# Local attention in chunks of 32 queries by 64 keys, one step per pair of heads, with a shifted copy of V by DMA

## The reference

```python
        def local_attention(q, k, v):            # 16 heads of 64, WINDOW = 32
            ...
            bk2, bv2 = (look(bk), look(bv))      # window before and own window: 64 keys
            ...
            mask = (it < jb) | (it > jb + w) | (jb == -1)
            sim = jnp.einsum('bhwie,bhwje->bhwij', bq, bk2) * QK_SCALE
            sim = jnp.where(mask, -jnp.finfo(sim.dtype).max, sim)
            attn = jax.nn.softmax(sim, -1)
            out = jnp.einsum('bhwij,bhwje->bhwie', attn, bv2)
        ...
        for i in range(DEPTH):
            x = attn_layer(shift_tokens(x), Wqkv[i], q_scale[i], k_scale[i], Wo[i]) + x
            x = ffn_layer(shift_tokens(x), ln_g[i], ln_b[i], W1[i], b1[i], W2[i], b2[i]) + x
```

## Time and profile before

| | |
|---|---|
| median of the runs | 5675.37 us |
| profiled execution | 5674.6 us, its span 5672.5 us |
| PE, PEld busy | 5156.9 us (91%), 3769.0 us (66%) |
| DVE, ACT, POOL busy | 4207.5 us (74%), 4014.1 us (71%), 2657.0 us (47%) |
| the two stretches of local layers | about 1040 to 3280 us and 3500 to 5672 us |

### The profile page before, as it was taken

The page is one execution under the profiler, slowest core; times in us unless marked ns, Lnnn a source line. Parts: engine busy times, 40 slices in busy tenths (PEclk is TensorE's granted clock), DMA queues, the critical chain, the costliest instruction groups (busy, mean ns, idle before and its releaser), DMA issues. The chain is left out here.

```text
span 5672.5 us, 176489 instructions
## 1 busy us (share of the span) xinstructions
PE 5156.9 (91%) x68706; PEld 3769.0 (66%) x68706; DVE 4207.5 (74%) x6500; ACT 4014.1 (71%) x7192; POOL 2657.0 (47%) x2485
## 2 busy tenths in 40 slices
PE   8997995799999999999998899799999999999998
PEld 3334432587777777777776433687777777777776
DVE  7885655687777777777776788687777777777775
ACT  5784664577777777777776578677777777777775
POOL 1100100465566665566654110475656665656663
PEclk8996997899999999999999899899999999999999
DMA  0000000100000000000000000100000000000000
GB/s 13 2 2 6 2 2 9 35 20 15 19 17 18 21 17 20 16 21 19 17 21 13 4 2 2 37 19 16 20 18 16 23 16 21 15 21 17 17 22 18
DMA packets 129243, 89.14 MB, mean 16 GB/s; under 512 B 33396, under 2 KB 122000, under 8 KB 128376
## 3 DMA queue, kind: packets, MB, share of 16 engines
q1 hardware_dynamic: 128376, 77.32, 4.9%
HBM read 69.54 MB, written 1.05 MB: 12 GB/s over the span
## 5 line engine op out<-in xcount | busy, mean ns | idle before, releaser
L1746 POOL TENSOR_TENSOR cross<-raw,tab_b 128x512 f32<-128x512 f32 x768 | 998.5, 1324 | 298.8 <-ACT raw L1612 295.5
L737 DVE TENSOR_REDUCE arena<-PS 128x1 f32<-128x512 f32 (+3 forms) x1408 | 828.9, 648 | 215.9 <-PE PS L550 130.4
L1752 POOL CAST kT_b<-kT 128x512 bf16<-128x512 f32 x384 | 349.5, 910 | 1199.2 <-ACT kT L1668 1198.1
L688 ACT ACTIVATE arena<-PS 128x1024 f32<-128x1024 f32 (+1 forms) x704 | 668.8, 968 | 200.7 <-PE PS L573 124.2
L1838 DVE TENSOR_TENSOR rot<-PS,tab_a 128x512 f32<-128x512 f32 x768 | 522.7, 687 | 330.7 <-ACT raw L1612 172.0
L1612 ACT COPY raw<-PS 128x512 f32<-128x512 f32 x768 | 448.1, 592 | 270.2 <-PE PS L1463 224.1
L1861 DVE TENSOR_TENSOR rot<-rot,inv_norm 128x1024 f32<-128x1024 f32 x384 | 561.8, 1463 | 47.7 <-ACT inv_norm L1628 37.8
L1867 DVE TENSOR_TENSOR oT<-PS,rec_den 128x384 f32<-128x384 f32 (+1 forms) x576 | 298.8, 519 | 369.3 <-ACT rec_den L1646 369.0
L1854 DVE TENSOR_TENSOR rot<-rot,cross 128x1024 f32<-128x1024 f32 x384 | 560.0, 1458 | 14.9 <-POOL cross L1746 13.7
L1442 PE MATMUL PS<-PT,V 128*64 128x96 f32 x8448 | 484.4, 256 | 76.2 <-DVE oT L1867 60.6
L1463 PE MATMUL PS<-w_qk_high,x_high 128*128 128x256 f32 x1536 | 478.0, 311 | 79.0 <-issue 34.0
(11 more groups left out here) (260 smaller groups left out, 12668.8 us busy)
## 6 DMA issues: line engine op xcount, KB each, us to landing
w_qk<-in_w_pairs SPq DMA_DIRECT2D x196, 128.0 KB, 2.1
w_v<-in_w_pairs SPq DMA_DIRECT2D x100, 128.0 KB, 2.2
w_o<-in_w_out_pairs SPq DMA_DIRECT2D x192, 64.0 KB, 1.9
xs<-staged SPq DMA_DIRECT2D x24, 224.0 KB, 2.5
w<-in_L_ffn_W SPq DMA_DIRECT2D x12, 341.0 KB
q_parts<-max_rows SPq DMA_DIRECT2D x192, 2.0 KB
V<-in_c_E SPq DMA_DIRECT2D x2, 896.0 KB, 7.9
w<-in_L_ffn_W SPq DMA_DIRECT2D x24, 64.0 KB
```

The source lines that it names most:

```text
L688: nc.scalar.activation(PT[u % 6].rearrange("p (a n) -> p a n", a=2)[:, :, first_q:512], PS[:, 2 * (u % 2):2 * (u % 2) + 2, first_q:512], A ...
L737: nc.vector.tensor_reduce(maxima[:, 2 * m + h, qt, kh:kh + 1], bank[:, 0:keys_of(qt, kh)], AX.X, ALU.max).then_inc(bank_free, 1)
L1746: nc.gpsimd.tensor_tensor(dst[:, :, :, o:o + 32], src[:, :, :, other:other + 32], tab[:, :, o:o + 32].unsqueeze(2).broadcast_to([128, 8, 2 ...
```

## The change

- Chunks are 32 queries by 64 keys. Four products of 64 keys by 32 queries lie in the array's four tiles at once; a pair has 64 such score products and 64 for the values. The mask and maximum products are 64 x 64, 32 of them, in the same four tiles.
- All chunks of a pair fill banks 4 and 5 completely (512 columns each), so there is one step: one `exps` of 1024 columns per partition, values in banks 6 and 7, the sums in banks 4 and 5, one Ln, one Exp and one `quotients` of 1024 columns. PT, log_den and rec_den are single buffers. Nothing of a pair's attention is left for the next position but what waits for it.
- V is kept at whole tiles of 128 tokens: four pieces, not six, 8 chunks, not 11. The keys of the even 32-query windows are V moved down by 32 partitions: SP makes this copy, `V_early`, by two DMAs in each even position, after `split_v`, after V3 is copied and after the last reader of the buffer. `values` waits for them (`v_moved`) in odd positions.
- The maxima go over blocks of 64 queries by 96 keys, in two groups of four.
- The order: Y0 and Y1 move from slots 0 and 1 to 1 and 2; V pieces stand in slots 5 and 1; X1 moves from slot 3 to 2; `inverse_norm`, `square`, `norms` and `normalise` are placed anew on ACT and DVE.

```diff
-QC = 96
-CHUNKS = -(-N // QC)
+QC = 32
+UNITS = N // 128
-KB = 80
+KB = 96
...
+        V_early = [own(f"V_early{m}", [128, UNITS, 256]) for m in range(2)]
...
             if yy:
-                names += {0: ["Y0"], 1: ["Y1"]}.get(slot, [])
+                names += {1: ['Y0'], 2: ['Y1']}.get(slot, [])
...
+                            taken_apart(sp, l, b, p, "V3")
+                            need_apart(sp, pv_full, it - 2)
+                            sp.dma_start(V_early[j % 2][32:128, :, :], V[j % 2][0:96, :, :]).then_inc(v_moved, 16)
+                            sp.dma_start(V_early[j % 2][0:32, 1:UNITS, :], V[j % 2][96:128, 0:UNITS - 1, :]).then_inc(v_moved, 16)
...
+                    for m in range(UNITS):
+                        for t in range(2):
+                            for w in range(2):
+                                for h in range(2):
+                                    rows, at = slice(64 * h, 64 * h + 64), 128 * m + 64 * w + QC * t
+                                    last = nc.tensor.matmul(PS[64 * w:64 * w + 64, 4 + h, 64 * m + QC * t:64 * m + QC * t + QC], kT[par][rows, at:at + 64],
+                                                            qT[par][rows, at:at + QC], start=False, stop=True,
+                                                            tile_position=(64 * h, 64 * w), skip_group_check=True)
...
+                def values(l, b, p, r):
+                    pair = (p + 7) % 8
+                    need(pe, exp_done, r + 1)
+                    need(pe, o_done, r)
+                    if p % 2 == 1:
+                        need(pe, v_moved, (r + 2) * 16)
...
@@ PE, position @@
-                    if oo:
-                        values(r - 1, NS - 1, (p + 6) % 8)
                     if bb:
                         maximum(l, b, p, 0)
                         maximum(l, b, p, 1)
...
                     if bb:
-                        scores(l, b, p, r, 0)
+                        scores(l, b, p, r)
                     late(l, b, p, 1)
-                    for s in range(NS - 1):
-                        if bb:
-                            scores(l, b, p, r, s + 1)
-                            values(r, s, (p + 7) % 8)
-                        late(l, b, p, s + 2)
+                    if bb:
+                        values(l, b, p, r)
+                    late(l, b, p, 2)
+                    late(l, b, p, 3)
                     late(l, b, p, 4)
```

More of the change, by code:

```diff
@@ L48, in shape_constants @@
     out = {"c_ident": np.eye(128, dtype=np.float32)}
[L50 to L57, removed]
-    out["c_E"] = E.reshape(128, -1)
[L60 to L63, removed]
+    j, q = np.arange(64)[None, :], np.arange(QC)[:, None]
+    E = np.zeros((2, 64, UNITS + 1, 64), np.float32)
+    E[:, 0:QC, :, :] = np.where((j >= q) & (j <= q + 32), 0.0, NEG)[None, :, None, :]
+    for unit in range(UNITS):
+        E[:, QC + unit, unit, :] = 1.0
+    E[:, QC, UNITS, :] = 1.0
+    E[:, QC + UNITS, UNITS, 0:32] = NEG
+    out["c_E"] = E.reshape(128, -1)
+    turn = np.zeros((128, 2, 64), np.float32)
+    turn[i, :, i % QC] = 1.0
+    turn[i % 64 < QC, :, QC + UNITS] = 1.0
+    out["c_turn"] = turn.reshape(128, -1)
+    blocks = np.zeros((128, 5, KB), np.float32)
+    i64, j96 = np.arange(64)[:, None], np.arange(KB)[None, :]
+    near = (j96 >= i64) & (j96 <= i64 + 32)
+    for c in range(5):
         for u in range(2):
-            blocks[64 * u:64 * u + 48, c, :] = np.where(near & (j80 >= 32) if c == 0 and u == 0 else near, 0.0, NEG)
+            blocks[64 * u:64 * u + 64, c, :] = np.where(near & (j96 >= 32) if c == 0 and u == 0 else near, 0.0, NEG)
     out["c_blocks"] = blocks.reshape(128, -1)
@@ L1166, in window_layers @@
         ff_cols, b2_row = own("ff_cols", [128, 8]), own("b2_row", [128, C])
[L1167 to L1170, removed]
+        E = own("E", [128, UNITS + 1, 64], BF16)
+        half_mask = [own(f"half_mask{m}", [128, 5, KB], BF16) for m in range(2)]
+        R, max_parts = own("R", [128, 128], BF16), own("max_parts", [128, 128], BF16)
         norms2 = [own(f"norms2_{m}", [128, 16]) for m in range(2)]
@@ new lines, in scores @@
+                                nc.tensor.matmul(PS[64 * w:64 * w + 64, 4 + h, 64 * m:64 * m + 64], E[rows, UNITS if (m, w) == (0, 0) else m, :],
+                                                 R[rows, 64 * w:64 * w + 64], start=m == 0, stop=True, tile_position=(64 * h, 64 * w), skip_group_check=True)
+                    for m in range(UNITS):
+                        for t in range(2):
[5 more added lines that the diff above has]
+                                                            tile_position=(64 * h, 64 * w), skip_group_check=True)
@@ L1432, in second_batch @@
                     pe.wait_ge(zeroed, ZEROED)
[L1433 to L1446 removed]
+                    pe.wait_ge(consts_made, 4)
```

228 lines of the change are left out of this document (101 added, 127 removed).

## The result

| | before | after |
|---|---|---|
| median of the runs | 5675.55 us (4 runs) | 5826.23 us (4 runs, 5816.15 to 5846.35) |
| ratio, 95% interval | | 1.0267 [1.0243, 1.0292] |
| profiled execution, its span | 5674.6, 5672.5 us | 5827.4, 5825.6 us |
| mean granted clock of PE | 0.960 | 0.922 |

Forecast: 5450 us, range 5290 to 5640, with 0.81 for faster. The change made the kernel 2.7% slower: the forecast was wrong in sign, and the range doesn't hold the time.

A forecast was written before the change was run, and what follows sets the result against it. PE was taken to bound positions 1, 2 and 5, DVE position 3, ACT position 4. Savings of 9.2 us over eight positions, times 24, made 221 us off 5674.6: 5454, forecast as 5450, range 5290 to 5640.

The forecast's parts named there:

- PE's sum per position: PE's attention work in one position: 6.1 us against 8.9 before, plus 0.5 less for V.
- 32 x 57 = 1.8 us: Float32 scores on PE: 32 groups of four records, each held 57 ns by its weight load; ends 0.9 and 2.7.
- The last rival: PE's clock falls with the new holes, said to be shorter than 2.3 us; given nothing of its own.
- The prediction's own sign of being wrong: Local clock under 0.95, listed with score groups over 3 us, PE waiting for V_early and longer positions.
- PE's saving: PE's work per position falls by 3.3 us: 2.8 in attention products and 0.5 in V products.
- the other waits: New PE idle time per position: 1.9 us between Q1 and the V piece, 0.3 before the scores, together 2.2.
- The shifted copy: The DMA copy of V to V_early lands at 8.6 us, 2 us before values in odd positions, hidden.
- The rival of the late copy: V_early lands 2.2 us late in 96 odd positions: up to +211 us, 5665 at worst, 5560 likelier; chance 0.16.
- x2 and x3 behind the second rotation: PE waits 1.3 to 1.8 us for DVE before the masks of x2 in nearly all positions.
- Float32 records at 25.6 ns each: Starting small products limits PE, so scores and values take 3.3 us each, not 1.8: 5960 us; chance 0.10.

The follow-up runs named there:

- e1: The after kernel without the two DMAs that copy V to V_early and the wait for them, so even windows read wrong keys: 5710.74 us.
- e2: The after kernel with the same V copy issued earlier, ahead of the wait for the split weights and the load of w_v: 5681.74 us.
- e3: The before kernel with four added DMAs in each even position, moving the same 1 MB inside SBUF to a buffer nobody reads: 5675.2 us.
- e5: e2 with a pair's sums, Ln, Exp and quotients moved to the start of the next position, and the second squares behind the exponential: 5547.1 us.
- e7: The before kernel with 64 more unread score products of the new small shape per position, in two stretches of 32: 5946.83 us.
- e10: The before kernel with the 64 extra score products of e7 all in one stretch: 6033.07 us.
- e11: The before kernel with 128 extra unread score products (256 records) per position in one stretch: 6778.61 us.
- e6: e5 with the scores cut in two halves around the V piece and the values around the pieces of slot 2: 5566.26 us.
- e4: e1 with the 64 score products of 32 columns made 32 of 64 columns, so the second half's scores are wrong: 5464.38 us.

## Why the prediction was wrong

- **The step that failed** is PE's sum per position, where it prices the small products by the array alone ("32 x 57 = 1.8 us") and takes PE as always fed. The sizes were right: 2.00 us for the scores (1.8 forecast), 1.89 for the values, 1.0 for the sums, wherever PE isn't stalled. But a run of these products is executed faster than its instructions arrive, and PE stands still 1.55 us more per position, 298 us in all. No row named in the prediction could show it: the longest run of small float32 products before was 32 records. What could have raised the question is PE's instruction queue on the page of before (packets, MB, share), which no term of the prediction uses:

```profile
q8 instruction: 576, 9.44, 0.7%
```

- **The clock.** The last rival gave the clock nothing, since "new holes are shorter than 2.3 us" and position 3 held 1.00. The holes are up to 4.5 us, and the low clock lasts 452 us longer. At most 226 us of the miss are this, about 180 by the second estimate. The prediction's own sign of being wrong, a local clock under 0.95, came (0.92).
- **PE's saving** of 3.3 us per position was too large even at the full clock, where 2.7 were measured: about 0.6, or 120 us. The small products aren't the reason; which term is, stays open.
- **The sum of it:** forecast -221, measured +153, a miss of 374 us. PE's work fell by 1.72 instead of 3.3 us: 303 us, of which some 180 are the clock and 120 the saving. Stalls add 298. Against them stand the other waits: the forecast passes on 1.15 of the 3.3 us (9.2 over eight positions), so it gives back 2.15, and 0.97 came: 227 us less. The 0.81 for faster left the stalls at nothing, and that the waits were charged too dear hid part of the miss by luck.
- **The shifted copy.** That it would be in time was right (9.7 us waited). That it would then be free was wrong: without it (e1) and with it elsewhere (e2) the kernel is 115 and 144 us faster, most of it in stalls and low clock, and e3 shows nothing for it where runs are short. The rival of the late copy had the right object and the wrong mechanism.
- **x2 and x3 behind the second rotation:** right, 183 waits of 1.2 us. e5 shows that this wait could have been filled, which, on top of the earlier copy, made a faster kernel of the change.
- **Float32 records at 25.6 ns each,** the rival on the other side, had 0.10. Its reason, that starting a record takes so long, is wrong (15.6 ns). Its number is near the 27 to 29 ns at which instructions arrive.
- **Two rules weighed.** For 128 float32 records in four tiles 15.6 ns each are measured, so the floor of about 25 ns of the Trainium skill, "TensorE: Matmul & The Clock Gate", section "Wait — 56ns, not 53.3ns?", doesn't hold here. The Trainium skill, "Runtime: NRT & Kernel Launch", section "Instruction fetch mechanics", says that instructions come in blocks of 16 KB, 256 of them, by a DMA queue of the engine, and that this is mostly hidden. The blocks agree with the packets (128 records, each with its weight load); that they are hidden holds for before and e7, but for some 35 us, and not for after, e10 and e11.

What stays open: the borders of the packets are the same in every layer of a loop, and the trace shows that an instruction packet is late behind a copy, but not by which mechanism, nor what sets its start where there is no transfer beside it. How much of the copy's cost is its traffic on the 16 engines and how much its delay of one packet wasn't tried apart. That instructions wait behind a transfer is read from the times of the packets; no run moved one packet alone. The price of the clock alone wasn't measured either.

## What to carry to other kernels

Price a run of small products twice: by the array, and by its instructions, one 16 KB packet per 128 float32 records (with their loads) and at best one about every 3.5 us. Where a run is cheaper by the array than that, keep it short: stretches of 64 records didn't stall (e7), runs of 128 did 54 times in 192 positions (e10), and nothing between was tried. Break it up with wide products that don't wait for anything new, or make fewer records, since one of 64 columns costs a tenth more than one of 32. Keep transfers from starting just ahead of a run. Charge a long hole twice, once for itself and once for the clock behind it; and before any engine is made faster, look for the next wait that the shorter work uncovers and put work into it.

## What the runs showed of the hardware

- PE waits for its own instructions, and the profile calls it only "issue". The end of a 16 KB packet of the instruction queue 1.27 to 1.55 us ahead of the next record gives it away (e5, e6, e11).
- In the first 3 us of after's 96 copies of 1 MB 3 instruction packets start, where the mean rate would give 43.
- A transfer of 1 MB beside a long run of small products lengthens such stalls (193.5 us to 108.0 at the scores when it is moved), and costs nothing otherwise (e3).
- At full clock a float32 record of a 64 x 64 tile takes 15.7 ns from start to start with 32 columns, 17.2 with 64 (e4) and 25.7 with 96 (before), four tiles in turn.
- After one hole of 4 us PE was granted 1.2 GHz for about 6 us while it was busy without a break. In e11 the holes, as long in sum as in after but in the small products of 2.0 us at most, left 388 us at the low clock against 604. The 54 holes of e10, of 1.3 us at most, left it where it was (156 us, before 152).
